# Attention and routed experts in one kernel: products of ones between lone scores, squares on ScalarE, one stack load and the end reordered

## What is computed

```python
xn = layernorm(x)                                   # over the 128 columns
out = x + attention(xn, Wq, Wk, Wv) + ffn(xn, ...)  # both read xn
# attention: 16 heads of 8 columns, q and k scaled by a factor that depends on the batch,
#            softmax(q k^T / sqrt(8)) v
# ffn: 32 experts of 64 hidden columns and one shared expert of 256
h = relu(x @ up_w[e].T) ** 2 * combine[:, e]        # combine: 6 of 32 experts for each row
moe = sum over e of h[e] @ down_w[e].T
shared = relu(x @ shared_up.T) ** 2 @ shared_down.T
```

## Time and profile before

| | |
|---|---|
| median of 3 runs | 664.43 us (664.24 to 665.41) |
| the profiled execution | 666.55 us, of which the span of the instructions 664.8 us |
| mean granted clock of TensorE | 0.981 |
| busy: TensorE | 645.4 us (97%) |
| busy: GpSimd (POOL) | 446.7 us (67%) |
| busy: VectorE (DVE) | 419.0 us (63%) |
| busy: ScalarE (ACT) | 410.0 us (62%) |
| DMA | 75.69 MB, 114 GB/s |

### The profile page before, as it was taken

How to read it: one execution, slowest core, us unless ns; L and a number is a source line. 1 busy time by engine, 2 the same in 40 slices (tenths; PEclk the granted TensorE clock), 3 DMA queues, 4 the chain that set the end, 5 groups by cost and what they waited for, 6 DMA issues and landing times.

```text
span 664.8 us, 12416 instructions
## 1 busy us (share of the span) xinstructions
PE 645.4 (97%) x4322; PEld 298.0 (45%) x4322; DVE 419.0 (63%) x1055; ACT 410.0 (62%) x785; POOL 446.7 (67%) x528
## 2 busy tenths in 40 slices
PE   8999699899999999999999999999999999999997
PEld 6433344444444444444444444444444444444453
DVE  7688556385756767575765757575765867565401
ACT  3457355476666666676667666665676667666653
POOL 6641648976788677876688667875766667566653
PEclk9679989999999999999999999999999999999999
DMA  4062834432546444253545534263544623332320
GB/s 137 5 209 68 241 95 100 137 130 61 138 100 223 97 101 108 71 198 86 144 101 180 140 65 114 69 220 96 128 101 109 189 75 108 76 88 65 97 65 17
DMA packets 51998, 75.69 MB, mean 114 GB/s; under 512 B 5984, under 2 KB 19168, under 8 KB 51936
## 3 DMA queue, kind: packets, MB, share of 16 engines
q1 hardware_dynamic: 51936, 74.90, 41.9%
HBM read 56.14 MB, written 18.35 MB: 112 GB/s over the span
## 4 chain that ended last, share of the span: by engine, by line
PE 89%; POOL 3%; DMA 2%; DVE 2%; SPq 2%; issue 1%; ACT 0%; POOLq 0%; DVEq 0%
PE acc L1060 22%; PE pv L1054 18%; PE upb L1111 16%; PE st L1024 12%; PE st L1029 5%; PE sc L1013 5%; PE upb L977 2%; PE upb L941 2%; PE upb L972 1%; DMA k_stack<-qk_parts 1%; PE upb L996 1%; DVE nmax L828 1%; POOL g L490 1%; POOL gated L486 1%; PE upb L936 1%
## 5 line engine op out<-in xcount | busy, mean ns | idle before, releaser
L828 DVE TENSOR_REDUCE nmax<-sc 128x1 f32<-128x512 f32 x512 | 328.8, 685 | 197.7 <-PE sc L1013 195.2
L620 ACT ACTIVATE probs<-st 128x512 f32<-128x512 f32 x512 | 277.6, 594 | 60.8 <-PE st L1029 60.3
L486 POOL TENSOR_TENSOR gated<-gate_at,relu 128x512 f32<-128x512 f32 x127 | 162.2, 1277 | 135.8 <-ACT relu L625 132.1
L490 POOL TENSOR_TENSOR g<-gated,relu 128x512 f32<-128x512 f32 x127 | 161.4, 1271 | 32.8 <-PE acc L1060 15.0
L1029 PE MATMUL st<-stacks 32*128 32x512 f32 x512 | 152.3, 580 | 0.0
L625 ACT ACTIVATE relu<-upb 128x512 f32<-128x512 f32 x128 | 76.4, 597 | 121.4 <-PE upb L1111 121.4
L1060 PE MATMUL acc<-dn,g 128*128 128x128 f32 x1016 | 146.7, 288 | 3.6 <-POOL g L490 3.6
L1060 PEld LDWEIGHTS acc<-dn,g 128*128 128x128 f32 x1016 | 123.1, 191 | 46.7 <-issue 43.6
L1054 PE MATMUL pv<-probs,v_aug 128*32 128x512 f32 x1024 | 138.1, 612 | 0.0
L1013 PE MATMUL sc<-stacks 32*128 32x512 f32 x512 | 134.9, 501 | 2.6 <-DVE nmax L828 2.5
L1111 PE MATMUL upb<-xnT,up 128*128 128x512 f32 x256 | 132.6, 600 | 0.3 <-ACT qk L567 0.3
(11 more groups left out here) (150 smaller groups left out, 421.8 us busy)
## 6 DMA issues: line engine op xcount, KB each, us to landing
gate_at<-gate_rows SPq DMA_DIRECT2D x62, 512.0 KB, 6.7
stacks<-q_stack SPq DMA_DIRECT2D x30, 256.0 KB, 5.0
stacks<-k_stack SPq DMA_DIRECT2D x30, 256.0 KB, 5.6
q_stack<-qk_parts SPq DMA_DIRECT2D x28, 256.0 KB, 6.5
k_stack<-qk_parts SPq DMA_DIRECT2D x28, 256.0 KB, 5.7
x_res<-in_x SPq DMA_DIRECT2D x8, 256.0 KB, 7.9
out<-y SPq DMA_DIRECT2D x8, 256.0 KB, 7.3
m_rows<-m_parts SPq DMA_DIRECT2D x96, 4.0 KB
```

What stands on the lines that cost most here:

```text
L486: nc.gpsimd.tensor_tensor(gated[:, u % 2, :], gate_at[:, group % RING, u % GATES, :], relu[:, u % RELUS, :], ALU.mult).then_inc(gated_read ...
L490: nc.gpsimd.tensor_tensor(g[:, u % 2, :], gated[:, u % 2, :], relu[:, u % RELUS, :], ALU.mult).then_inc(g_ready, 1)
L620: nc.scalar.activation(probs[:, u % 2, h, :], st_b[h % 2][:], ACT.Exp).then_inc(probs_ready, 1)
L828: nc.vector.tensor_reduce(out=nmax[:, s % 2, at:at + 1], in_=sc_b[tile % SC_BANKS][:], op=ALU.max, axis=AXX, negate=True).then_inc(s_read, 1)
```

## The change

It has five parts.

1. Products of ones (`warm`) are put between scores: five after each of the pairs 1, 3 and 5 of the start, three after the first, second and fourth of the six scores of step 1, and two before each of the ten scores of units 0 and 1. They are 15, 9 and 20 products.
2. In batch 0 (units 0 to 15) ScalarE squares the relu in place (`square_relu(u - 1)`, at the end of unit u), and GpSimd multiplies once, gate by square. It waits for the square (`sq_ready`).
3. SP loads batch 1's first stack no longer ahead of the third set of max rows, but behind it; for that it waits for all weight products of step 1 as well.
4. The last batch's residual is no longer added by TensorE. VectorE adds the attention to `x_res` in two halves (`add_pair`), the second behind the last division, and the last sum takes `x_res`.
5. `pv(127)` stands before `expert_down(126)`, and the last transposition before `expert_down(127)`.

```diff
+        WARM_PAIR, WARM_AHEAD, WARM_UNIT = {1: 5, 3: 5, 5: 5}, {0: 3, 1: 3, 3: 3}, 2
+        WARM_UNITS = range(2)
...
@@ the loop of the sync engine over the steps s @@
                     load_max(s + 1)
+                    if s == 1:
+                        sp.wait_ge(t_done, (s + 1) * TILES)
+                        load_stack(1, 0)
                     if s == 0:
                         store_gates(0)
                         load_gates(0)
...
                 if j == 3 and b + 2 < B:
                     store_parts(b + 2)
+                if s == 0:
+
+                    continue
                 if b + 1 < B:
-                    sp.wait_ge(t_done, (s + 1) * TILES)
+                    if s > 1:
+                        sp.wait_ge(t_done, (s + 1) * TILES)
                     load_stack(b + 1, j)
...
@@ GpSimd @@
             def gating(u):
                 group = u // GATES
-                pool.wait_ge(relu_ready, u + 1)
+                if u < SLICES:
+                    pool.wait_ge(sq_ready, u + 1)
+                else:
+                    pool.wait_ge(relu_ready, u + 1)
...
+                if u < SLICES:
+
+                    wait(pool, down_done, u - 1)
+                    nc.gpsimd.tensor_tensor(g[:, u % 2, :], gate_at[:, group % RING, u % GATES, :],
+                                            relu[:, u % RELUS, :], ALU.mult).then_inc(g_ready, 1)
+                    return
...
-                pool.wait_ge(gated_ready, u + 1)
+                pool.wait_ge(gated_ready, u - SLICES + 1)
...
@@ ScalarE @@
+            def square_relu(u):
+
+                act.wait_ge(relu_ready, u + 1)
+                at = relu[:, u % RELUS, :]
+                nc.scalar.activation(at, at, ACT.Square).then_inc(sq_ready, 1)
...
                 exponent(u, 2)
                 exponent(u, 3)
+                if 0 < u <= SLICES:
+                    square_relu(u - 1)
             att_evac(STEPS // PAIR - 1)
...
@@ VectorE @@
+            def add_pair(k):
+
+                if k == 0:
+                    dve.wait_ge(x_res_ld, B * 16)
+                dve.wait_ge(atty_ready, B * NQ - (PAIR if k == 0 else 0))
+                columns = slice(k * PAIR * QUAD * HD, (k + 1) * PAIR * QUAD * HD)
+                nc.vector.tensor_tensor(x_res[:, :, columns], x_res[:, :, columns],
+                                        att_y[:, :, k * PAIR:(k + 1) * PAIR, :].rearrange("p t j c -> p t (j c)"), ALU.add
+                                        ).then_inc(x_added, 1)
+
             def last_sum():
-
-                dve.wait_ge(atty_ready, B * NQ)
+                dve.wait_ge(x_added, PAIR)
                 dve.wait_ge(down_done, B * SLICES)
                 dve.wait_ge(y_stored, (B - 1) * 16)
-                nc.vector.tensor_tensor(y[:, 1, :], acc_b[:], att_y[:].rearrange("p t j c -> p (t j c)"),
+                nc.vector.tensor_tensor(y[:, 1, :], acc_b[:], x_res[:].rearrange("p t d -> p (t d)"),
                                         ALU.add).then_inc(y_ready, 1)
...
+            add_pair(0)
             last_gating()
             att_out(STEPS // PAIR - 1)
+            add_pair(1)
             last_sum()
...
@@ TensorE, couple(u, k) @@
                 for tile in SC_AT[u, k]:
+                    if u in WARM_UNITS:
+
+                        warm(WARM_UNIT, acc_b)
                     score(tile)
...
@@ TensorE, before the units @@
                 score(2 * i + 1)
                 if i in BESIDE:
                     beside(*BESIDE[i])
+                else:
+                    warm(WARM_PAIR[i], st_b[1])
...
                 score(TILES + i)
                 if i in BEHIND:
                     beside(*BEHIND[i])
+                elif i in WARM_AHEAD:
+                    warm(WARM_AHEAD[i], acc_b)
...
@@ TensorE, the units and the end @@
                     shared_down(b, SHDOWN_UNIT.index(n))
-                if u == UNITS - TT:
-                    add_x()
                 if u == UNITS - 1:
                     expert_up(u)
...
+            pv(UNITS - 1)
+
             for u in range(UNITS - LAG, UNITS - 1):
                 expert_down(u)
-            pv(UNITS - 1)
-            expert_down(UNITS - 1)
             pe.wait_ge(relu_ready, UNITS)
             att_transpose(STEPS // PAIR - 1)
+            expert_down(UNITS - 1)
```

More of the change, by code:

```diff
@@ L202, in build @@
         up_done = sem("up_done"); relu_ready = sem("relu_ready")
-        gated_ready = sem("gated_ready"); g_ready = sem("g_ready")
+        sq_ready = sem("sq_ready"); gated_ready = sem("gated_ready"); g_ready = sem("g_ready")
         sh_done = sem("sh_done"); sh_relu = sem("sh_relu"); sh_ready = sem("sh_ready")
@@ L206, in build @@
         sum_ready = sem("sum_ready"); y_ready = sem("y_ready")
-        last_gated = sem("last_gated"); last_g = sem("last_g")
+        last_gated = sem("last_gated"); last_g = sem("last_g"); x_added = sem("x_added")
         ATT_KT, MAX_KT, CUT_KT = 1, 2, 1
@@ L1073, in expert_down @@
                 down_slice(src, dn[:, n, :], n == 0, n == SLICES - 1).then_inc(down_done, 1)
[L1075 to L1080, removed]
             def shared_down(b, i):
```

## The result

The change takes **672.75 us** (median of 4 executions, 671.74 to 673.75) against 664.38 before (664.24 to 665.41): ratio 1.0123, 95% interval 1.0104 to 1.0141. It is 1.2% slower, clear of the noise, and outside the range that was given. The profiled execution took 672.48, span 670.7, and stands at the median.

A forecast was written before the change was run, and what follows sets the result against it. TensorE, 97% busy, was taken as the bound, with half-clock stretches and waits for `m_rows`, `g` and a maximum. Terms 5.6 - 2.9 - 3.2 - 0.85 - 0.3 = -1.65 gave a median of 662.8 us, range 657.2 to 667.0.

The forecast's parts named there:

- Part 1, the start of unit 2: Products of ones up to unit 2: unit 2 starts 5.6 us later, ends 4.5 and 9.
- its own signs of being wrong: Included a start shift under 4 or over 8 us, and `m_rows` landing 2 us after issue.
- The gain of the 15 products: In the start, ahead of `max_transpose(0)`: full clock brings it from 29.05 to 27.0, a gain of 2.0 us.
- Units 0 and 1 at full clock: Units 0 and 1 with their 20 products: 15.7 us at full clock against 11.1 before, a loss of 4.6.
- Rival C: Units 0 and 1: clock falls nevertheless, after the idle 1.1 us; start costs 9, result 666.2 us; chance 0.19.
- Part 3: `m_rows` for unit 8, issued behind `x_next`, land at about 79.9 instead of 82.8: -2.9 us, ends -1.5 and -6.5.
- Rival B: At unit 8, `m_rows` pass the stores: -6.5 for -2.9, clock up -3.0, new stack wait 0.8; 657.0 us; chance 0.12.
- Rival A: At unit 8, the shorter wait leaves the clock up: 662.8 - 3.0 = 659.8 us; chance 0.17.
- Part 2: Squares on ScalarE, batch 0: waits for `g` and half a late maximum go, -3.2 us, ends -1.8 and -4.0.
- Add_x: Near the end, `add_x` leaves TensorE's chain and the couple behind it pays 0.56 instead of 0.32: -0.85 us.
- The end: The last sum starts at 661.05 instead of 661.35: -0.3 us, ends 0 and -0.6.
- the change moves both alike: Profiled execution, 2.1 us above the median before, and median shift equally: 664.9 profiled gives a median of 662.8.

The follow-up runs named there:

- e2: The changed kernel without any of its 44 products of ones, parts 2 to 5 as changed: 657.14 us, ratio 0.9902 to before.
- e8: The whole change with 4 products of ones put into the 1.09 us pause ahead of unit 0: 664.44 us, ratio 0.9992 to before.
- e5: e3 with the stack load put back ahead of the third max rows (part 3 undone): 657.80 us, ratio 0.9905 to before.
- e7: e3 with 4 products of ones put into the 1.09 us pause ahead of unit 0: 651.57 us, ratio 0.9809 to before.
- e12: e7 plus 10 products in unit 8's wait and its `m_rows` issued from ScalarE's queue: 648.79 us, ratio 0.9766 to before.
- e13: e12 without the 10 products of ones in the wait at unit 8: 650.02 us, ratio 0.9769 to before.
- e1: The changed kernel without its 20 products of ones in units 0 and 1: 655.78 us, ratio 0.9887 to before.
- e4: The kernel before with only the 44 products of ones added: 680.68 us median; executions 672.23, 671.81, 689.13, 690.75.
- e3: The changed kernel with only the 15 products of the start, none in the six scores or units 0 and 1: 654.87 us, ratio 0.9868.

## Why the prediction was wrong, step by step

**Part 1, the start of unit 2: +5.6 forecast, +16.1 measured.** This is the step that failed, by 10.5 us: the prediction took units 0 and 1 at full clock, and the clock fell behind the pause ahead of them. A start shift of over 8 us was among its own signs of being wrong. In it:

- `max_transpose(0)` at 26.54 (27.0 forecast), the six scores with their products +3.4 (+3.1), unit 0 +0.9 (+1.1): near enough. The gain of the 15 products was counted as fixed, though: against the 26.83 of e2, which has none, it is 0.3.
- Units 0 and 1 at full clock: 17.3 us for my 15.7. A pair with its score takes 1.07 (0.65 + 0.43 in e8), for which I took 0.93. Behind a score two products take 0.65 us, three 0.87 (27.12 to 27.99 in the change's timeline) and five 1.31 (17.36 to 18.67): 0.22 for each and 0.21 once for the group. I had used a rate for each and nothing for the group. Ten times 0.14 is 1.4 of the 1.6, and three groups of three explain the 3.4 above (2.6 + 0.86).
- The sentence "now, at full clock" is what cost the rest. The clock fell behind the 1.1 us pause, and all that stands in units 0 and 1 was paid at half clock: 26.3 for 17.3, 9.0 us. Rival C named this mechanism with its place, and e8 shows it right. But it was priced with the 7 us and the 3.5 of work of the kernel before, and its 9 doesn't add up even so: 5.6 + 0.9 + 3.5 is 10.0. With the clock down until unit 1 is nearly done, all of the added work is paid at that rate, 1.15 a pair. Priced so, C gives 5.6 + 1.6 + 9.0 = 16.2 at unit 2, and 662.8 + 10.6 = 673.4 at the end.

**Part 3: -2.9 forecast, -3.6 measured** from the storing of the gates (58.91 to 74.62, +15.7) to unit 8 (+12.1), and 3.1 in e5 against e7. Right, and for the reason given: `m_rows` land 0.3 us behind `x_next`. Rival B, that they pass the stores, doesn't happen in one queue; in another it does (e12, e13), and its new wait for the stack in unit 9, forecast at 0.8, is 1.45. The clock behind the wait was counted at nothing, with the other end at -3.0: it gave 1.3, from +12.1 to +10.8, since the stretch at 0.50 went from 6.8 us to 3.2. Rival A didn't come about: in all eight profiles with a wait of 2.98 us or more at unit 8 (before, the change, e1, e2, e4, e5, e7, e8) the clock fell in the wait or within 2 us of its end. In e3 it stayed up, behind a shorter wait:

```profile
76.58 0.39 PE L1063 MATMUL st<-m_rows,ones 3*128 3x512 bf16 x2 [2.27 <-DMA m_rows<-m_parts]
```

**Part 2: -3.2 forecast, -3.7 measured** (-4.1 between units 9 and 17; +0.4 in unit 18, where a score waits for its maximum at 150.13, which it overlapped before). The cover held: the idle time ahead of relu went from 121.4 to 115.1.

**Add_x: -0.85 forecast, -0.86** (631.05 to 655.28 is 24.23, now 638.12 to 661.49, 23.37).

**The end: -0.3 forecast, -0.3 measured.** From the last couple to the last sum 6.07 us before, 5.79 now. `pv(127)` comes 0.74 earlier, with one `expert_down` less ahead of it and 0.28 of wait; the second add takes back 0.46.

The sum of what was measured: 16.1 - 0.4 (units 2 to 5) - 3.6 - 1.3 - 3.7 - 0.9 - 0.3 = 5.9 between the profiled executions. The profile of before stands 2.1 above its median and that of after 0.3 below its own, so the medians differ by 8.4. Here was a second error: I took it that the change moves both alike. The profile of before had a mean clock of 0.981; executions of that kernel at 0.985 took 663.7 to 665.1. So what lifted it was clock, and that is what the change touches.

## What to carry to other kernels

Filler work for the clock paid here in the pauses: 1 us in a pause of 1.1 us gave 3 us (e7 for e3) and 8 or more on top of the change, while the same products inside units 0 and 1 cost 0.44 us each at full clock and 0.70 with the clock down, and did not bring it back. In the start, between scores that wait for VectorE, they kept the clock up, for a gain of 0.2 to 2.4 us. Before costing anything that is added behind a pause, cost it at half clock too, and carry that as the rival's price. Where executions differ by their clock, compare landmarks of traces, or executions at the same mean clock, before the median of a few is read.

## What the hardware did that was not expected

- A granted clock of 0.50 for 20, 47 and 54 us in a row with TensorE busy in all of them (20.00 of 20.00, 47.00 of 47.00, 54.00 of 54.00). Nothing but the work of units 0 to 5 and products of ones or data stood in them. In the kernel before such stretches had lasted 7 to 10 us.
- One program has outcomes of 664.7, 672 and 682 us, with mean clocks of 0.994, 0.981 and 0.962; e4 has 672 and 690, with 0.993 and 0.960.
- The clock fell behind a pause of 1.09 us (ahead of unit 0, in eight profiles of ten) and stayed up behind one of 2.27 (e3, at unit 8): the length of the pause alone doesn't tell.
- Small transfers from another engine's queue passed a full queue (e13), and still took 5 to 8 us for 4 KB each.
